# Four gate and value products of an attention chunk, from one float32 matmul each to three passes over split operands

## The chip, the cores and the metric

The kernel runs on one core of a Trainium2 chip. TensorE (PE) multiplies, VectorE (DVE), ScalarE (ACT) and GpSimd (POOL) do elementwise work, and SyncE (SP) issues transfers. The metric is the device time of one execution in microseconds, lower is better. Three runs of the kernel before gave 1155.25 us as the median (1154.32 to 1161.18).

## What is computed

Eight chunks of 512 tokens by 128 features pass through two model layers. Layer 0 is a feed-forward part with LoRA experts, a gated attention, and the same feed-forward part again; layer 1 is a mixture of experts, a softmax attention, and the mixture again. The change is in layer 0's attention, whose core is:

```python
h = _layernorm(x, ln1_g, ln1_b)
v = h @ Wv + bv
log_f = log_sigmoid(h @ Wf + bf);  log_i = log_sigmoid(h @ Wi + bi)
o = sigmoid(h @ Wo + bo)
scores = exp(log_i^T + cumsum(log_f) - cumsum(log_f)^T + causal)
attn = (scores / (sum(scores) + 1e-6)) @ v
x = x + o * attn;  x = x + mlp(layernorm(x))
```

The kernel computes the scores' two sums as scans along the tokens: `den` from the two gates, `num` from the gates and the values.

## The kernel before, in words

**Slots.** Layer 0 is written out by hand in slots. Slot `m` does the main feed-forward work of one chunk in one of the two feed-forward parts (m = 0 to 15), and beside it one step each of other chunks: chunk `m - 3` is at its gates (`a_gate`), chunk `m - 4` at its normalisation (`a_norm`), chunk `m - 5` at the first half of its small MLP (`a_up`), chunk `m - 6` at the second (`a_down`), and from m = 9 on chunks are sorted for the experts of layer 1 (`r_...`). So the gates run in slots 3 to 10. Every engine has its own list of steps per slot; the order within an engine is fixed by that list, and semaphores tie the engines together. A slot of the middle takes some 45 us. After the slots, from about 680 us on, come the experts and the softmax attention of layer 1, which the change does not touch.

**The passes.** `mm3` already does the feed-forward products in three matmuls of the type float32r (a shorter float that is kept in four bytes): the high part of the weights by the high and by the low part of the moving operand, then the low part of the weights by the high part. All other products are plain float32 matmuls, which the trace shows as two records each.

**The gates.** In slot `m`, PE transposes the normalised chunk into the shared bank `BSIDE` early in the slot (`a_T`), ACT evicts it with scale and bias to `hT`, and PE reads `hT` near the end of the slot, in four products into the same bank (`a_gate(0)` to `a_gate(3)`: input gate, forget gate, output gate, values). ACT evicts three of them with a sigmoid (`a_gates`); DVE reads the fourth in `a_scans`, which runs the `den` scan, the product `iv` and the `num` scan. Other PE steps stand between the gates: `up(1)` and half of `value(0)`, then `down(2)` and `down(3)`.

**The shared bank.** In the next slot PE's `a_den`, eight tiny matmuls (1x1), turns the row `den` into columns in that bank. It waits for the `num` scan and for the `hT` eviction of the following chunk, since that empties the bank. Behind it on PE stand `h(3, 2)`, `pre_T` and `a_back`. ACT evicts what `pre_T` writes (`tT` and its rounded copy), then normalises into `h2` (`a_mid_norm`), and DVE's `a_mix` waits for that; so DVE's work of the slot starts from there.

**DVE and POOL.** DVE's `act(k)` are two operations, bank by `sil` and then `act` by the mask `wT`. POOL adds (`total`), takes differences and raises the variances to the power -1/2 (`a_mid_scale` and others). DVE's `a_leaky(0)` late in the slot is followed on ACT by `a_square(0)`, `a_mid(2)`, `mask(2)`, `mask(3)`; PE's `up(0)` waits for `mask(3)`, DVE's `masked(0)` for `up(0)` and for POOL's `mask_diff`. 

Of the kernel before, what the change touches and what calls it, by code (L numbers as in the profile page):

```python
# [69 lines left out]
def build(nc, d, out):  # L70
    with ExitStack() as ctx:
        def sb(name, shape, dt=F32):
            return ctx.enter_context(nc.sbuf_tensor(name, shape, dt))

        def sem(name, per_item=1):
            return Sem(ctx.enter_context(nc.semaphore(name)), per_item)
# [10 lines left out]
        bank = [ctx.enter_context(nc.psum_tensor(f"bank{i}", [P, S], F32)) for i in range(8)]  # L87
# [9 lines left out]
        vecs = sb("vecs", [P, 8]); bif = sb("bif", [P, 2]); wif = sb("wif", [P, 2])  # L97
        wi_b = sb("wi_b", [P, P]); wf_b = sb("wf_b", [P, P])
        wv = sb("wv", [P, P]); wo = sb("wo", [P, P])
# [20 lines left out]
        gsum = [sb(f"gsum{i}", [P, S]) for i in range(2)]  # L120
        r1 = sb("r1", [P, S]); r2 = sb("r2", [P, S]); oT = sb("oT", [P, S])
        w1, w3, b1, b3 = act_[0]
# [6 lines left out]
        hT = sb("hT", [P, S])  # L129
        gi = sb("gi", [P, S]); gf = sb("gf", [P, S]); go = sb("go", [P, S])  # L130
        iv = sb("iv", [P, S]); num = sb("num", [P, S]); den = sb("den", [P, S]); oaT = sb("oaT", [P, S])
        denc = sb("denc", [P, 2, T])
# [4 lines left out]

        lower = sb("lower", [P, P]); lower_bf = sb("lower_bf", [P, P], BF16); ones_bf = sb("ones_bf", [P, P], BF16); ones = sb("ones", [P, 1])
        token_i = sb("token_i", [P, NCH * T], I32); token = sb("token", [P, NCH * T])
# [33 lines left out]
        mxr = sb("mxr", [P, 2]); nmx = sb("nmx", [P, 2]); rs = sb("rs", [P, 2]); rsi = sb("rsi", [P, T])  # L173

        with nc.sbuf_tensor("split", [P, 29 * S], F32R) as split:
            def parts(n, width=S):
                return tuple(split[:, (n + k) * S:(n + k) * S + width] for k in range(2))
            w1s, w3s, b1s, b3s = parts(0), parts(2), parts(4), parts(6)
            a1s, a3s = (tuple(split[:, 8 * S + (k + i) * P:8 * S + (k + i + 1) * P] for k in range(2)) for i in (0, 2))
            ts = [parts(9), parts(11)]  # L180
            uas = [[parts(13 + 8 * p + 2 * i) for i in range(2)] for p in range(2)]
            uds = [[parts(17 + 8 * p + 2 * i) for i in range(2)] for p in range(2)]
# [21 lines left out]
        routing_constants, ranked, zrow_ready, rows_zeroed = sem("routing_constants", 8 + E), sem("ranked"), sem("zrow_ready"), sem("rows_zeroed")  # L204
        prod_ready, prod_saved, scaled, spread, weight_high, weight_low = (
            sem("prod_ready"), sem("prod_saved"), sem("scaled"), sem("spread"), sem("weight_high"), sem("weight_low"))

# [9 lines left out]

        bn_a, stat_a, rstd_a, normed_a, ynT_a, hT_saved = (
            sem("bn_a", 4), sem("stat_a"), sem("rstd_a", 2), sem("normed_a", 2), sem("ynT_a"), sem("hT_saved"))
        gates_ready, gates_saved, scan_steps, oa_ready = sem("gates_ready", 4), sem("gates_saved", 3), sem("scan_steps", 3), sem("oa_ready")  # L220
# [39 lines left out]

        SPLITS = [(a1s, a1, 1.0), (a3s, a3, 1.0), (w1s, w1[:, :], 1.0), (b1s, b1[:, :], LORA), (w3s, w3[:, :], 1.0), (b3s, b3[:, :], LORA)]

        def window(eng, row, first, n, most):
# [89 lines left out]
        def _(pe):  # L353
# [22 lines left out]
            def first_layer(s):  # L376
# [215 lines left out]
                def a_gate(i):  # L592
                    n = s.a_gate
                    if n is None:
                        return
                    pe.wait_ge(*hT_saved(n))
                    if i == 0:
                        if n == 0:
                            pe.wait_ge(spread.sem, 2)
                        if s.a_norm is not None:  # L600
                            pe.wait_ge(*z_ready(s.a_norm))
                        if s.a_down is not None:
                            pe.wait_ge(*xa_done(s.a_down))
                        if s.a_up is not None:
                            pe.wait_ge(*m_saved(s.a_up))
                        if s.r_pre is not None:
                            pe.wait_ge(*xnT_saved(s.r_pre))
                    else:
                        pe.wait_ge(*gates_saved(n, i))
                    mm(bank[BSIDE][:, :], (wi_b, wf_b, wo, wv)[i][:, :], hT[:, :], start=True, stop=True).then_inc(gates_ready.sem, 1)  # L610

# [165 lines left out]
        def _(act):  # L777
# [12 lines left out]
            def first_layer(s):  # L790
# [128 lines left out]
                def a_T():  # L919
                    n = s.a_gate  # L920
                    if n is None:
                        return
                    if n == 0:
                        act.wait_ge(weights_loaded.sem, 16 * len(loads))
                        for k, w in enumerate((wi_b, wf_b)):
                            af(w[:, :], wif[:, k:k + 1].to_broadcast([P, P]), ACT.Copy).then_inc(spread.sem, 1)
                    act.wait_ge(*ynT_a(n))
                    act.wait_ge(*gates_ready(n - 1))
                    af(hT[:, :], bank[BSIDE][:, :], ACT.Identity, bias=vecs[:, 1:2], scale=vecs[:, 0:1]).then_inc(hT_saved.sem, 1)

# [133 lines left out]
        def _(dve):  # L1064
# [28 lines left out]
            def first_layer(s):  # L1093
# [163 lines left out]
                def a_scans():  # L1257
# [249 lines left out]
        def _(pool):  # L1507
# [13 lines left out]
            def first_layer(s):  # L1521
# [73 lines left out]
                def a_product():  # L1595
# [135 lines left out]
```

## Time and profile before

| | |
|---|---|
| median of three runs | 1155.25 us (1154.32 to 1161.18) |
| the profiled execution | 1153.79 us, of it span 1152.1 us |
| PE busy | 969.3 us (84%) |
| DVE, ACT, POOL busy | 721.7, 498.7, 494.9 us |
| mean granted TensorE clock | 0.928 of 2.4 GHz |

The page of the profile has one line of tenths for each engine, in 40 slices of 28.8 us. PE stands at nine tenths in slices 2 to 23, that is through the slots. A PE record is longer than the step to the next one, since matmuls overlap in the array; so distances between starts are read here, not lengths. A value in brackets behind a row is the idle time of that engine just before it, and who ended it.

### The profile page before, as it was taken

Reading aid. Unit: us, or ns where it says so; the run is one execution under the profiler, and the core shown is the slowest. Engines: PE = TensorE matmul, PEld = TensorE weight load, DVE = VectorE, ACT = ScalarE, POOL = GpSimd, SP = SyncE. Lnnn points to the kernel's source line nnn. Section 1 sums busy time; section 2 is a strip of 40 time slices with the busy share of each in tenths; the row PEclk is TensorE's granted clock in tenths of the full one; section 3 lists DMA queues with packets and bytes.
Section 4 is the critical chain, followed back from the end, with each engine's and each line's share of the span. In section 5 each row is a group of like instructions: output and inputs, shape, how many; then the busy total and the mean of one; then the engine's idle time right before and its main releaser. Section 6 shows DMA issues by size and latency. Waiting matters only on the chain. (4 is left out here: it accounts for less than half of the span.)

```text
span 1152.1 us, 15196 instructions
## 1 busy us (share of the span) xinstructions
PE 969.3 (84%) x4224; PEld 674.8 (59%) x4224; DVE 721.7 (63%) x2206; ACT 498.7 (43%) x1007; POOL 494.9 (43%) x475
## 2 busy tenths in 40 slices
PE   3999999999999999989999975888488884448884
PEld 2666655656656556556667644777255563337663
DVE  4878777868778777777878753444345546534332
ACT  3433454655565565634533322444144453323441
POOL 2445555455454453536545652444400005724434
PEclk9999999999999999999999976999789995569997
DMA  5087000000000000000000022555400000125441
GB/s 165 1 345 295 1 1 0 1 1 1 1 1 1 1 1 1 1 1 10 3 8 10 11 72 64 172 155 163 125 21 1 1 1 17 38 63 170 147 142 49
DMA packets 42901, 65.11 MB, mean 57 GB/s; under 512 B 7154, under 2 KB 25122, under 8 KB 40641
## 3 DMA queue, kind: packets, MB, share of 16 engines
q1 hardware_dynamic: 37824, 55.59, 14.7%
q0 software_dynamic: 4992, 8.54, 2.2%
q8 instruction: 35, 0.57, 0.2%
q14 instruction: 50, 0.40, 0.1%
HBM read 37.20 MB, written 28.74 MB: 57 GB/s over the span
## 5 line engine op out<-in xcount | busy, mean ns | idle before, releaser
L362 PE MATMUL bank<-split 128*128 128x512 f32 x416 | 207.4, 498 | 15.7 <-ACT wT L837 8.3
L364 PE MATMUL bank<-split 128*128 128x512 f32 x416 | 165.4, 398 | 0.0
L363 PE MATMUL bank<-split 128*128 128x512 f32 x416 | 165.1, 397 | 0.0
L798 ACT ACTIVATE sil<-bank 128x512 f32<-128x512 f32 x128 | 76.6, 599 | 114.5 <-PE bank L364 106.6
L1537 POOL TENSOR_TENSOR gsum<-act 128x512 f32<-128x512 f32 x64 | 84.9, 1327 | 89.5 <-DVE act L1109 89.5
L412 PE MATMUL bank<-act,a 128*128 128x512 f32 x256 | 117.9, 593 | 0.0
L362 PEld LDWEIGHTS bank<-split 128*128 128x128 f32 x416 | 79.5, 191 | 58.9 <-issue 20.4
L714 PE MATMUL bank<-hT_e,e 128*128 128x256 f32 x368 | 93.0, 397 | 20.0 <-ACT hT_e L1015 18.9
L1105 DVE TENSOR_TENSOR act<-bank,sil 128x512 f32<-128x512 f32 x128 | 87.8, 686 | 21.2 <-PE bank L364 19.3
L363 PEld LDWEIGHTS bank<-split 128*128 128x128 f32 x416 | 79.9, 192 | 29.0 <-issue 18.8
L698 PE MATMUL bank<-xlT,e 128*128 128x256 f32 x368 | 92.3, 396 | 3.3 <-ACT xlT L1002 2.7
L1109 DVE TENSOR_TENSOR act<-act,wT 128x512 f32<-128x512 f32 x128 | 90.0, 703 | 4.4
L364 PEld LDWEIGHTS bank<-split 128*128 128x128 f32 x416 | 79.4, 191 | 18.3
L714 PEld LDWEIGHTS bank<-hT_e,e 128*128 128x128 f32 x368 | 68.1, 195 | 33.9 <-ACT hT_e L1015 24.4
L1651 POOL DMA_INDIRECT out<-ob,ids x46 | 45.2, 983 | 80.0 <-DVE ob L1446 71.1
L1651 POOL DMA_INDIRECT rows_out<-ob,ids x46 | 45.2, 983 | 76.5 <-DVE ob L1446 68.7
L1007 ACT ACTIVATE ob<-xin 128x128 f32<-128x128 f32 x92 | 40.3, 485 | 86.8 <-DMA out<-ob,ids 44.2
L698 PEld LDWEIGHTS bank<-xlT,e 128*128 128x128 f32 x368 | 69.7, 199 | 13.5 <-ACT xlT L1002 3.9
L412 PEld LDWEIGHTS bank<-act,a 128*128 128x128 f32 x256 | 47.7, 191 | 42.3 <-issue 34.9
L1640 POOL DMA_INDIRECT rows_in<-yw,slot_i x64 | 63.0, 984 | 21.0 <-issue 15.5
L1438 DVE TENSOR_SCALAR oT_e<-bank,eb2T 128x256 f32<-128x256 f32 x46 | 22.3, 484 | 79.3 <-PE bank L714 79.3
L422 PE MATMUL bank<-gsum,w 128*128 128x512 f32 x128 | 65.2, 599 | 0.5 <-POOL gsum L1537 0.5
(280 smaller groups left out, 1926.2 us busy)
## 6 DMA issues: line engine op xcount, KB each, us to landing
e<-e_dram SPq DMA_DIRECT2D x92, 256.0 KB, 3.1
rows_in<-yw SPq DMA_DIRECT2D x17, 1056.0 KB, 17.9
xin<-rows_in SPq DMA_DIRECT2D x46, 132.0 KB, 3.1
x<-rows_out SPq DMA_DIRECT2D x8, 256.0 KB, 4.7
rows_in<-yw,slot_i POOLq DMA_INDIRECT x64, 2.3
rows_out<-ob,ids POOLq DMA_INDIRECT x46, 2.3
out<-ob,ids POOLq DMA_INDIRECT x46, 2.3
act<-b_dram SPq DMA_DIRECT2D x2, 256.0 KB, 3.2
```

What stands on the lines that cost most here:

```text
L362: mm(dst, w[0], m[0], start=start, stop=False, **more)
L363: mm(dst, w[0], m[1], start=False, stop=False, **more)
L364: return mm(dst, w[1], m[0], start=False, stop=stop, **more)
L412: last = mm(bank[BV][:, :], a2[:, j, :], act_[e][j][:, :], start=j == 0, stop=j == J - 1)
L422: mm(bank[BOUT][:, :], w2[:, j, :], gsum[j % 2][:, :], start=j == 0, stop=False).then_inc(w2_used.sem, 1)
L698: last = mm(bank[2 * p + j // 2][:, (j % 2) * Q:(j % 2 + 1) * Q], w[:, rows(j)], xlT[p][:, :], start=True, stop=True)
L714: last = mm(bank[4][:, 0:Q], w[:, j, :], hT_e[p][:, j, :], start=j == 0, stop=j == J - 1)
L798: af(sil[(k - 1) % 2][:, :], bank[BH1[STEPS[k - 1][0] % 2]][:, :], ACT.Silu).then_inc(silu_done.sem, 1)
L1105: v.tensor_tensor(a[:, :], bank[BH3[j % 2]][:, :], sil[(k - 1) % 2][:, :], ALU.mult).then_inc(act_done.sem, 1)
L1109: v.tensor_tensor(a[:, :], a[:, :], wT[g % 2][e][:, :], ALU.mult).then_inc(weighted.sem, 1)
L1537: pool.tensor_tensor(out=gsum[j % 2][:, :], in0=act_[0][j][:, :], in1=act_[1][j][:, :], op=ALU.add).then_inc(summed.sem, 1)
L1651: pool.indirect_dma_start((rows_out, o)[n3 // NT], bass.IndirectOffsetOnAxis(ids[n3 % 4][:, q:q + 1], 0), ob[n3 % 4][:, q, :], None, bound ...
```

## The change

Each of the four gate and value products becomes `mm3`. The four weights are split once, in slot 3, by four ACT copies (the high parts, where two copies stood that spread the gates' weight columns) and four DVE operations (`gates_low`). The moving operand is split for each chunk: ACT evicts the bank a second time, rounded, into the first half of `hT_split`, and signals `hT_saved` only after that; POOL subtracts in a new step `a_low`, between `a_mid_scale` and `total(1)`. `hT_split` lies on the memory of `iv` and `r2`, so ACT's eviction now waits for the `num` scan of the chunk before. The gates wait for `hT_low`.

```diff
-        wi_b = sb("wi_b", [P, P]); wf_b = sb("wf_b", [P, P])
+        gates_w = sb("gates_w", [P, 8 * P], F32R)
...
+        with nc.sbuf_tensor("hT_split", [P, 2 * S], F32R) as hT_split:
+            hTs = hT_split[:, 0:S], hT_split[:, S:2 * S]
+        iv, r2 = sb("iv", [P, S]), sb("r2", [P, S])
...
+        GATES = [wif[:, k:k + 1].to_broadcast([P, P]) for k in range(2)] + [wo[:, :], wv[:, :]]
...
-                    pe.wait_ge(*hT_saved(n))
+                    pe.wait_ge(*hT_low(n))
...
-                    mm(bank[BSIDE][:, :], (wi_b, wf_b, wo, wv)[i][:, :], hT[:, :], start=True, stop=True).then_inc(gates_ready.sem, 1)
+                    mm3(bank[BSIDE][:, :], gate_w[i], hTs, True, True).then_inc(gates_ready.sem, 1)
...
-                        for k, w in enumerate((wi_b, wf_b)):
-                            af(w[:, :], wif[:, k:k + 1].to_broadcast([P, P]), ACT.Copy).then_inc(spread.sem, 1)
+                        for dst, w in zip(gate_w, GATES):
+                            af(dst[0], w, ACT.Copy).then_inc(gate_high.sem, 1)
                     act.wait_ge(*ynT_a(n))
                     act.wait_ge(*gates_ready(n - 1))
-                    af(hT[:, :], bank[BSIDE][:, :], ACT.Identity, bias=vecs[:, 1:2], scale=vecs[:, 0:1]).then_inc(hT_saved.sem, 1)
+                    act.wait_ge(*scan_steps(n - 1))
+                    for dst in (hT[:, :], hTs[0]):
+                        last = af(dst, bank[BSIDE][:, :], ACT.Identity, bias=vecs[:, 1:2], scale=vecs[:, 0:1])
+                    last.then_inc(hT_saved.sem, 1)
...
+                def gates_low():
+                    if s.a_gate != 0:
+                        return
+                    dve.wait_ge(weights_loaded.sem, 16 * len(loads))
+                    for n, (dst, w) in enumerate(zip(gate_w, GATES)):
+                        dve.wait_ge(gate_high.sem, n + 1)
+                        v.scalar_tensor_tensor(dst[1], w, 1.0, dst[0].bitcast(F32), ALU.mult, ALU.subtract).then_inc(gate_low.sem, 1)
...
                 r_rows(s.r_sort, BSIDE)
+                gates_low()
                 masked(0)
...
+                def a_low():
+                    n = s.a_gate
+                    if n is None:
+                        return
+                    pool.wait_ge(*hT_saved(n))
+                    if l is not None:
+                        pool.wait_ge(*r_ready(l))
+                    pool.tensor_tensor(out=hTs[1], in0=hT[:, :], in1=hTs[0].bitcast(F32), op=ALU.subtract).then_inc(hT_low.sem, 1)
...
                 a_mid_scale()
+                a_low()
                 total(1)
```

How the order changes is seen best on three engines. On PE, before, from the second gate of slot 3 to the next slot's first product:

```order
L610 MATMUL bank<-hT,wf_b 128x512 [waits gates_saved,hT_saved]
L422 MATMUL bank<-gsum,w 128x512 [waits summed]
L610 MATMUL bank<-hT,wo 128x512 [waits gates_saved,hT_saved]
L422 MATMUL bank<-gsum,w 128x512 [waits summed]
L610 MATMUL bank<-hT,wv 128x512 [waits gates_saved,hT_saved]
L362 MATMUL bank<-split 128x512 [waits silu_done,t_low]
```

The same place now:

```order
L367 MATMUL bank<-hT_split,gates_w 128x512 [waits gates_saved,hT_low]
L368 MATMUL bank<-hT_split,gates_w 128x512
L369 MATMUL bank<-hT_split,gates_w 128x512
L427 MATMUL bank<-gsum,w 128x512 [waits summed]
L367 MATMUL bank<-hT_split,gates_w 128x512 [waits gates_saved,hT_low]
L368 MATMUL bank<-hT_split,gates_w 128x512
L369 MATMUL bank<-hT_split,gates_w 128x512
L427 MATMUL bank<-gsum,w 128x512 [waits summed]
L367 MATMUL bank<-hT_split,gates_w 128x512 [waits gates_saved,hT_low]
L368 MATMUL bank<-hT_split,gates_w 128x512
L369 MATMUL bank<-hT_split,gates_w 128x512
L367 MATMUL bank<-split 128x512 [waits silu_done,t_low]
```

Each gate is three instructions in the place of one, and nothing else moved. On ACT, at the start of a slot, before (`L798` is `silu`, `L929` the eviction, `L808` and `L809` are `pre_T`'s two evictions, `L862` is `a_mid_norm`):

```order
L798 ACTIVATE sil<-bank 128x512 [waits h1_ready]
L929 ACTIVATE hT<-bank,vecs 128x512 [waits gates_ready,ynT_a]
L798 ACTIVATE sil<-bank 128x512 [waits act_done,h1_ready]
L808 ACTIVATE tT<-bank,normw 128x512 [waits h3_ready,t_low,ynT_f]
L809 ACTIVATE split<-bank,normw 128x512
L862 ACTIVATE h<-z,nb_z,sc_z 128x128 [waits h2T_ready,rstd_z]
```

and now:

```order
L803 ACTIVATE sil<-bank 128x512 [waits h1_ready]
L936 ACTIVATE hT<-bank,vecs 128x512 [waits scan_steps,gates_ready,ynT_a]
L936 ACTIVATE hT_split<-bank,vecs 128x512
L803 ACTIVATE sil<-bank 128x512 [waits act_done,h1_ready]
L813 ACTIVATE tT<-bank,normw 128x512 [waits h3_ready,t_low,ynT_f]
L814 ACTIVATE split<-bank,normw 128x512
L867 ACTIVATE h<-z,nb_z,sc_z 128x128 [waits h2T_ready,rstd_z]
```

The eviction has a second instruction and a further wait. On POOL, before, in the first third of a slot (`L1537` is `total`, `L1591` and `L1593` are `a_mid_scale`):

```order
L1537 TENSOR_TENSOR gsum<-act 128x512 [waits w2_used,weighted]
L1591 TENSOR_TENSOR sc_z<-sc_z,neghalf 128x4 [waits stat_z]
L1593 TENSOR_TENSOR nb_z<-sc_z,mv_z 128x4 [waits rstd_z]
L1537 TENSOR_TENSOR gsum<-act 128x512 [waits w2_used,weighted]
L1550 TENSOR_TENSOR sc_f<-sc_f,neghalf 128x4 [waits stat_f]
```

and now:

```order
L1554 TENSOR_TENSOR gsum<-act 128x512 [waits w2_used,weighted]
L1608 TENSOR_TENSOR sc_z<-sc_z,neghalf 128x4 [waits stat_z]
L1610 TENSOR_TENSOR nb_z<-sc_z,mv_z 128x4 [waits rstd_z]
L1628 TENSOR_TENSOR hT_split<-hT,hT_split 128x512 [waits r_ready,hT_saved]
L1554 TENSOR_TENSOR gsum<-act 128x512 [waits w2_used,weighted]
L1567 TENSOR_TENSOR sc_f<-sc_f,neghalf 128x4 [waits stat_f]
```

The new subtraction stands between `nb_z` and the second `total`.

## Rows read from the trace of the kernel before

**Rows 1.** The page, busy time by engine (us, share of the span, instructions):

```profile
PE 969.3 (84%) x4224; PEld 674.8 (59%) x4224; DVE 721.7 (63%) x2206; ACT 498.7 (43%) x1007; POOL 494.9 (43%) x475
```

**Rows 2.** Who waited for whom, PE, 160 to 485 us (total, times, longest):

```profile
PE bank L362 <- ACT wT L837: 5.4, 7, 2.5
PE bank L610 <- ACT gi L903: 2.0, 5, 0.4
PE bank L362 <- DVE ud L1173: 1.5, 1, 1.5
```

**Rows 3.** Timeline of PE, end of slot 7 (start, length, engine, line, operation):

```profile
328.76 1.88 PE L412 MATMUL bank<-act,a 128*128 128x512 f32 x4
330.47 1.02 PE L610 MATMUL bank<-hT,wi_b 128*128 128x512 f32 x2
...
334.29 1.10 PE L610 MATMUL bank<-hT,wf_b 128*128 128x512 f32 x2 [0.39 <-ACT gi L903]
...
338.22 1.10 PE L610 MATMUL bank<-hT,wv 128*128 128x512 f32 x2
...
339.39 0.40 PE L363 MATMUL bank<-split 128*128 128x512 f32 x1
339.62 0.40 PE L364 MATMUL bank<-split 128*128 128x512 f32 x1
...
343.85 1.05 PE L492 MATMUL bank<-ones,den 1*128 1x1 f32 x8
```

**Rows 4.** Timeline of ACT, slot 7 and the start of slot 8:

```profile
324.70 0.63 ACT L894 ACTIVATE msq<-msq 128x512 f32<-128x512 f32 x1 [0.63 <-DVE msq L1247]
...
326.13 0.60 ACT L835 ACTIVATE wT<-bank 128x512 f32<-128x512 f32 x1 [0.22 <-PE bank L467]
...
332.16 1.28 ACT L903 ACT_TABLE_LOAD   x1
...
335.42 0.69 ACT L903 ACTIVATE gf<-bank,bif 128x512 f32<-128x512 f32 x1 [1.28 <-PE bank L610]
...
342.57 0.78 ACT L929 ACTIVATE hT<-bank,vecs 128x512 f32<-128x512 f32 x1
```

**Rows 5.** Timeline of DVE, the scans at the same place:

```profile
339.41 1.62 DVE L1265 TENSOR_TENSOR_SCAN den<-gf,gi 128x512 f32<-128x512 f32 x1 [4.78 <-PE bank L610]
...
341.71 1.49 DVE L1268 TENSOR_TENSOR_SCAN num<-gf,iv 128x512 f32<-128x512 f32 x1
```

**Rows 6.** Timeline of DVE and POOL, two overlaps, in slots 11 and 7:

```profile
488.20 1.27 POOL L1529 TENSOR_TENSOR split<-tT,split 128x512 fp32r<-128x512 f32 x1 [3.26 <-ACT split L809]
488.34 1.68 DVE L1109 TENSOR_TENSOR act<-act,wT 128x512 f32<-128x512 f32 x1
...
308.59 1.26 POOL L1584 TENSOR_TENSOR x<-x,z 128x512 f32<-128x512 f32 x1
308.75 1.12 DVE L1078 SCALAR_TENSOR_TENSOR part_z<-part_z 128x4 f32<-128x4 f32 x1
```

**Rows 7.** Timeline of POOL and DVE, where the subtraction is put, slots 7 and 4:

```profile
313.90 0.20 POOL L1593 TENSOR_TENSOR nb_z<-sc_z,mv_z 128x4 f32<-128x4 f32 x1
314.38 0.69 DVE L1109 TENSOR_TENSOR act<-act,wT 128x512 f32<-128x512 f32 x1
...
181.89 1.30 POOL L1537 TENSOR_TENSOR gsum<-act 128x512 f32<-128x512 f32 x1
183.50 0.15 DVE L1163 TENSOR_TENSOR dlt<-mx 128x4 f32<-128x4 f32 x1
```

**Rows 8.** Timeline of PE in slot 10, and a stretch (PEclk is the granted clock):

```profile
435.75 1.02 PE L492 MATMUL bank<-ones,den 1*128 1x1 f32 x8 [1.00 <-ACT hT L929]
...
437.14 0.63 PE L363 MATMUL bank<-split 128*128 128x512 f32 x1
437.57 0.63 PE L364 MATMUL bank<-split 128*128 128x512 f32 x1
...
437.00:443.00 6.00, 6.00 (x20) 4.12 (x20) 2.39 (x6) 2.63 (x6) 1.27 (x1) 0.72 0.00 0
```

More of the change, by code:

```diff
@@ L97, in build @@
         vecs = sb("vecs", [P, 8]); bif = sb("bif", [P, 2]); wif = sb("wif", [P, 2])
-        wi_b = sb("wi_b", [P, P]); wf_b = sb("wf_b", [P, P])
+        gates_w = sb("gates_w", [P, 8 * P], F32R)
+        gate_w = [tuple(gates_w[:, (2 * i + k) * P:(2 * i + k + 1) * P] for k in range(2)) for i in range(4)]
         wv = sb("wv", [P, P]); wo = sb("wo", [P, P])
@@ L120, in build @@
         gsum = [sb(f"gsum{i}", [P, S]) for i in range(2)]
-        r1 = sb("r1", [P, S]); r2 = sb("r2", [P, S]); oT = sb("oT", [P, S])
+        r1 = sb("r1", [P, S]); oT = sb("oT", [P, S])
         w1, w3, b1, b3 = act_[0]
@@ L130, in build @@
         gi = sb("gi", [P, S]); gf = sb("gf", [P, S]); go = sb("go", [P, S])
-        iv = sb("iv", [P, S]); num = sb("num", [P, S]); den = sb("den", [P, S]); oaT = sb("oaT", [P, S])
+        num = sb("num", [P, S]); den = sb("den", [P, S]); oaT = sb("oaT", [P, S])
         denc = sb("denc", [P, 2, T])
@@ L136, in build @@
         mv_z = sb("mv_z", [P, T]); sc_z = sb("sc_z", [P, 2, T]); nb_z = sb("nb_z", [P, T])
-        lower = sb("lower", [P, P]); lower_bf = sb("lower_bf", [P, P], BF16); ones_bf = sb("ones_bf", [P, P], BF16); ones = sb("ones", [P, 1])
+        lower = wak; lower_bf = sb("lower_bf", [P, P], BF16); ones_bf = sb("ones_bf", [P, P], BF16); ones = sb("ones", [P, 1])
         token_i = sb("token_i", [P, NCH * T], I32); token = sb("token", [P, NCH * T])
@@ L204, in build @@
         routing_constants, ranked, zrow_ready, rows_zeroed = sem("routing_constants", 8 + E), sem("ranked"), sem("zrow_ready"), sem("rows_zeroed")
-        prod_ready, prod_saved, scaled, spread, weight_high, weight_low = (
-            sem("prod_ready"), sem("prod_saved"), sem("scaled"), sem("spread"), sem("weight_high"), sem("weight_low"))
+        prod_ready, prod_saved, scaled, gate_high, gate_low, weight_high, weight_low = (
+            sem("prod_ready"), sem("prod_saved"), sem("scaled"), sem("gate_high"), sem("gate_low"), sem("weight_high"), sem("weight_low"))
         bn_f, stat_f, rstd_f, normed_f, ynT_f = sem("bn_f", 4), sem("stat_f"), sem("rstd_f"), sem("normed_f"), sem("ynT_f")
@@ L216, in build @@
         out_ready, outT_saved, back_ready, xf_done = sem("out_ready"), sem("outT_saved"), sem("back_ready"), sem("xf_done")
-        bn_a, stat_a, rstd_a, normed_a, ynT_a, hT_saved = (
-            sem("bn_a", 4), sem("stat_a"), sem("rstd_a", 2), sem("normed_a", 2), sem("ynT_a"), sem("hT_saved"))
+        bn_a, stat_a, rstd_a, normed_a, ynT_a, hT_saved, hT_low = (
+            sem("bn_a", 4), sem("stat_a"), sem("rstd_a", 2), sem("normed_a", 2), sem("ynT_a"), sem("hT_saved"), sem("hT_low"))
         gates_ready, gates_saved, scan_steps, oa_ready = sem("gates_ready", 4), sem("gates_saved", 3), sem("scan_steps", 3), sem("oa_ready")
@@ L595, in a_gate @@
                         return
-                    pe.wait_ge(*hT_saved(n))
+                    pe.wait_ge(*hT_low(n))
                     if i == 0:
                         if n == 0:
-                            pe.wait_ge(spread.sem, 2)
+                            pe.wait_ge(gate_low.sem, 4)
                         if s.a_norm is not None:
```

## The prediction

> **What bounds the kernel now.** I read the page first: PE is busy 84% of the span [rows 1], and the tenths show nine or more all through the slots, the only part that the change touches. A busy PE is not yet a bound, so the second view is PE's list of waits over slots 4 to 10 (160 to 485 us): some 10 us in 325 [rows 2, 8]. The reader should see that PE is the bound there, and that it still waits at four places: at `up(0)` for the masks on ACT (`L837`), at the second gate for the first sigmoid (`L903`), once for DVE's `ud`, once at `a_den` for `hT`. A delay is paid in full at each place where PE waits already, or where the slack is smaller than the delay. Third come the timelines around the gates and `a_den` [rows 3 to 5], fourth those around the place where POOL gets its new operation [rows 6, 7].
>
> **The gates.** A float32 product takes 0.855 us of PE (two of them from 328.76 to 330.47), a float32r pass 0.23 us (339.39 to 339.62) [rows 3], so three passes take 0.69 us and 32 products save at most 32 x 0.165 = 5.3 us. Not all of it counts:
> - The first gate's saving is lost. The second gate waits for the first sigmoid, that one for its table load at 332.16 [rows 4], which stands on ACT behind the last square or `up_high(0)`, and not behind the gate. Only in slot 5, by the same view, does the load start right after the gate: -0.14 us.
> - The second and third gate are each followed by their sigmoid, on which the next gate waits: 334.29 to 338.22 is two periods of 1.96 us [rows 3]. From the gate's start to its sigmoid it is 1.13 us now (335.42 [rows 4]). With three passes it is about 0.33 + 0.23 to the start of the last one, 0.40 for its record, 0.03 to ACT: 0.99. Saved 2 x 0.14 in 8 slots: -2.2 us.
> - The fourth gate belongs to the next term.
>
> Sum **-2.4 us**, with ends -5.3 and -1.
>
> The Trainium skill (FP8 and Floating Point Precision, TensorE Precision Notes) says that true float32 takes four passes through the array, so three would take three quarters. By that the product would fall to 0.64 us, an estimate from that page, and the gates would give about 0.8 us more. The trace's passes are 0.23 apart, for their weight loads are in the stream too, and the sum goes by the trace.
>
> **The wait at `a_den`.** Now `a_den` starts 5.63 us after the fourth gate of the slot before (338.22 to 343.85 [rows 3]); it is just about not waiting, since `hT` was done at 343.35 [rows 4]. In the new kernel: 0.99 us from the gate's start to the scans (1.19 now, 339.41), 3.79 to the end of the `num` scan (341.71 + 1.49 = 343.20) [rows 5], 0.05 to ACT, which waits for it now, 0.68 for `hT` (0.78 less a tenth of overlap between neighbours), 0.78 for the second eviction [rows 4], 0.13 back to PE. Sum 6.42 us, 0.79 more than now. Six slots (4 to 9): +4.7. In slot 10 ACT is late on its own account (PE waits 1.00 us there already [rows 8]), so the second eviction adds 0.68. In slot 11 there is no eviction, and the scans come 0.2 sooner. Sum **+5.2 us**. What is queued behind `a_den` on PE is `h(3, 2)`, `pre_T` and `a_back`, and `pre_T` feeds the chain over ACT to `a_mix`, from which DVE's slot starts; so nothing absorbs it: both the bound engine and its follower shift. Lower end: if the scan wait were free, `a_den` could start 0.68 after today's 343.48, at 344.16, 0.3 late, less the 0.2 of the gate: +1 us in all. Upper end: the full 1.0 us seven times, +7.
>
> **POOL's subtraction.** It takes 1.27 us like its neighbours, and POOL has room. But in this trace a DVE operation whose inputs both lie in SBUF stands still while a POOL operation on 512 columns runs: `L1109` took 1.68 instead of 0.69 us when POOL had started 0.14 earlier, and a tiny `L1078` 1.12 [rows 6], where `L1163`, as small, takes 0.15 [rows 7]. The subtraction starts at 314.12, behind `nb_z`; `L1109` follows at 314.38 [rows 7], would stand until 315.39 and end at 315.94 in place of 315.07: +0.87 us on DVE. In slots 4 and 5 the subtraction falls on DVE work that reads PSUM, but it pushes `total` from 181.89 to 183.19, over `L1163` at 183.50 [rows 7]: +0.95. In slot 3, where nothing stands between the first `total` and the subtraction, the same reading gives 0.45.
>
> What of it reaches PE: DVE's chain runs without a gap up to `a_leaky(0)`, and behind that ACT has `a_square(0)`, `a_mid(2)` and the masks on which `up(0)` waits. In slots 3, 4 and 5 PE or DVE waits on that chain already (the 1.5 us in slot 4, the longest, 2.5 us, in slot 5 [rows 2]): 0.45 + 0.95 + 0.95. In slot 7 the masks have 0.22 us of slack [rows 4], and the same reading of the others gives 0 in slot 6, 0.2 in 8 and 9, 0.57 in 10: 0.9 + 0.6 + 0.7 + 0.5 + 0.25. Together 5.3 us. `gates_low`, four small operations before `masked(0)` in slot 3, would be hidden by DVE's wait for `mask_diff`, but falls on that very POOL operation: +0.4 us. Sum **+5.7 us**. Lower end 0, if the starts fall apart by the 0.26 us that decide it, upper 8 times 1.0.
>
> The Trainium skill (SBUF — State Buffer, Who interferes with whom) has this as an exclusive lock: whichever starts first keeps it for the whole instruction. By that rule, were `L1109` to start first, DVE would lose nothing there, and POOL would end 0.7 us later; but then `total` comes over `L1163`, as in slot 4, and DVE pays its 0.95 after all. No row shows that order.
>
> **The clock.** In slot 10 PE stood still for 1.00 us, did 1.0 us of 1x1 matmuls, and its passes came 0.43 us apart behind that, at a granted clock of 1.2 GHz; the mean from 437 to 443 us is 0.72 [rows 8]. The new stall at `a_den` makes nearly the same picture in slots 4 to 9. A fall costs what that one did: seven passes or transposes at 0.43 instead of 0.23, about 1.5 us. Whether it falls depends on how stall and clock happen to lie; slot 5 shows one fall after 2.5 us, slot 4 none after 1.5. I take two of six: **+3.0 us**, ends 0 and 9.
>
> **Hidden.** Two more ACT copies and 0.2 us each in slot 3 lie in a gap of 1 us before `hT`. The second silu of a slot comes 0.7 us later, and what needs it waits for `h(3, 2)`, which comes 1 us later. Semaphore waits that are met already cost no gap in these rows. Nothing after 680 us changes.
>
> **Sum.** -2.4 + 5.2 + 5.7 + 3.0 = +11.5 us on the profiled execution's 1153.8: **1165 us**. That execution stands 1.5 us below the median of the three runs. A change of under 1% (11.6 us) can't be told from none in this kernel.
>
> **Rivals.**
> - *The collisions fall apart or are absorbed, and the clock holds.* Against the sum: the port's 0.26 us margin. For it: half the waits that POOL's operation brings would be shadowed by the stall at `a_den`, if PE's delay exceeds DVE's. -2.4 + 5.2 + 3 = +6, 1157 to 1162 us. Chance 0.27.
> - *Slower by more than 1%: the clock falls at most stalls.* Place: behind `a_den` in slots 4 to 10; price 1.5 us each, at six 9 us: 1171 us. It decides from four falls on. For it: slot 10 shows the same pattern with the fall. Against: the other long waits did not all bring one. Chance 0.16.
> - *The passes win.* Place: the gates. If ACT's second eviction and the wait for the scan hid behind `h(1, 2)`, and the port did not matter, the gates' -2.4 to -5.3 would stand alone: 1149 to 1152, up to 1156 with a little of the rest. Against it: `a_den` has no slack to hide 0.8 us in. Chance 0.12.
>
> The forecast has 0.45. Its own range is 1162 to 1168. Holding 8 in 10 takes the first rival's upper part and the second's lower: **1156 to 1172 us**. Faster by over 1% would need 11.5 us, twice what all gates can give: 0.02. Slower by over 1% (above 1166.8) takes the second rival and a third of the forecast: 0.31. Within 1%: 0.67.
>
> **What the profile afterwards would show.** PE's list of waits has `a_den` behind ACT's `L936` in slots 4 to 10 with 0.9 us each, 6 to 7 us in total. The distance from a gate's first pass to its sigmoid is near 1.0 us, and from sigmoid to sigmoid 1.82. `L1109`'s successor beside the subtraction takes about 1.5 us, and DVE's `dlt` 1.1 in slots 4 and 5. The wait of `up(0)` for the masks grows from 5.4 to 9 us or more. Clock: two falls more between 160 and 430 us. The prediction fails if the eviction starts before the `num` scan ends, if the DVE operations keep their 0.69 us, or if PE makes up for the stall later in the slot.

## The result, and the profile after

The changed kernel takes 1169.65 us (1165.53 to 1171.15, 4 runs) beside 1155.26 (1154.32 to 1161.18, 4 runs): ratio 1.0108, interval 1.0065 to 1.0151. The profiled execution took 1170.37 us, its span 1168.6. Ratios are to the kernel before on the same chip, with a 95% interval. In a row of a wait, the three numbers are the total in us, how often, and the longest.

PE's line of the page beside [rows 1]: the 32 further instructions are the three passes (a float32 matmul counted as two records).

```profile
PE 976.3 (84%) x4256; PEld 685.7 (59%) x4256; DVE 728.4 (62%) x2210; ACT 504.0 (43%) x1017; POOL 505.7 (43%) x483
```

Who waited for whom, PE, 160 to 485 us (beside [rows 2]):

```profile
PE bank L497 <- ACT hT_split L936: 8.1, 7, 1.7
PE bank L367 <- ACT wT L842: 6.0, 7, 2.1
PE bank L367 <- ACT gi L908: 2.3, 4, 0.6
PE bank L367 <- DVE ud L1181: 1.8, 1, 1.8
```

One line is new and large, `a_den` (`L497`) behind the second eviction, seven times. The masks' line hardly grew. The end of slot 7, timeline of all engines (beside [rows 3 to 5]):

```profile
342.34 0.47 PE L367 MATMUL bank<-hT_split,gates_w 128*128 128x512 f32 x1 [0.61 <-ACT gi L908]
...
343.31 0.69 ACT L908 ACTIVATE gf<-bank,bif 128x512 f32<-128x512 f32 x1 [1.12 <-PE bank L369]
...
344.14 0.47 PE L367 MATMUL bank<-hT_split,gates_w 128*128 128x512 f32 x1
...
345.95 0.47 PE L367 MATMUL bank<-hT_split,gates_w 128*128 128x512 f32 x1
...
346.40 1.30 POOL L1582 TENSOR_TENSOR split<-ua,split 128x512 fp32r<-128x512 f32 x1 [3.28 <-ACT split L851]
...
346.98 1.81 DVE L1273 TENSOR_TENSOR_SCAN den<-gf,gi 128x512 f32<-128x512 f32 x1 [4.52 <-PE bank L369]
...
349.47 1.49 DVE L1276 TENSOR_TENSOR_SCAN num<-gf,iv 128x512 f32<-128x512 f32 x1
...
351.07 0.78 ACT L936 ACTIVATE hT<-bank,vecs 128x512 f32<-128x512 f32 x1 [0.78 <-DVE num L1276]
...
351.75 0.77 ACT L936 ACTIVATE hT_split<-bank,vecs 128x512 fp32r<-128x512 f32 x1
...
352.66 1.02 PE L497 MATMUL bank<-ones,den 1*128 1x1 f32 x8 [1.06 <-ACT hT_split L936]
```

The gates come 1.80 us apart (1.96 before) and a gate reaches its sigmoid in 0.97 us (1.13). ACT now waits for the scan, evicts twice, and PE has stood still for 1.06 us. POOL and DVE in the same slot, and DVE in slot 4 (beside [rows 6, 7]):

```profile
186.41 0.89 DVE L1171 TENSOR_TENSOR dlt<-mx 128x4 f32<-128x4 f32 x1
...
321.54 1.30 POOL L1628 TENSOR_TENSOR hT_split<-hT,hT_split 128x512 fp32r<-128x512 f32 x1
321.86 1.53 DVE L1117 TENSOR_TENSOR act<-act,wT 128x512 f32<-128x512 f32 x1
```

`L1117`, the multiplication by the mask (`L1109` before), takes 0.84 us more than alone; about 1.5 us was foreseen, 1.53 came. `dlt` takes 0.74 us more, where 0.95 was foreseen. The 6 us behind each `a_den` of slots 4 to 10 (stretch, length, busy PE, PEld, DVE, ACT, POOL, then the granted clock):

```profile
168.00:174.00 6.00, 5.66 (x24) 4.68 (x25) 4.21 (x12) 1.95 (x4) 0.26 (x1) 0.72 0.01 3
212.00:218.00 6.00, 5.80 (x24) 4.52 (x25) 3.39 (x8) 2.71 (x7) 0.82 (x1) 0.72 0.00 0
259.00:265.00 6.00, 5.56 (x28) 4.07 (x29) 3.62 (x9) 3.26 (x8) 1.24 (x2) 1.00 0.01 3
306.00:312.00 6.00, 5.96 (x29) 4.23 (x30) 3.23 (x8) 3.18 (x7) 1.27 (x1) 1.00 0.01 3
352.00:358.00 6.00, 5.34 (x23) 4.53 (x24) 3.85 (x9) 2.25 (x5) 0.33 (x1) 0.72 0.01 3
400.00:406.00 6.00, 5.65 (x24) 4.61 (x25) 3.77 (x10) 2.35 (x6) 0.32 (x1) 0.72 0.01 3
448.00:454.00 6.00, 5.28 (x23) 4.50 (x24) 3.71 (x14) 1.88 (x4) 0.00 (x0) 0.72 0.01 3
```

A stretch of full speed has 1.00; 0.72 is the mean of a stretch that spends a part of its 6 us at 1.2 GHz. So the clock falls behind `a_den` in five of seven. In the trace of before only slot 10 shows it [rows 8]. Each of the two traces has one more fall in slot 5, late in the slot (at 236 and 242 us), which does not stand behind `a_den`.

**The measure for all runs.** `a_den` stands once in each slot on PE, so the distance between two of its starts is the price of a slot. I read it from each trace; the medians then say whether the sum holds. Slot 7 to 8 is the clean one: only the rows marked * have a fall of the clock in it. The column "slots 4 to 11" runs from `a_den` of slot 4 to that of slot 11.

| kernel | slot 7 to 8 | slots 4 to 11 | median us (runs) | ratio, interval |
|---|---|---|---|---|
| before | 45.32 | 316.76 | see text | 1 |
| changed | 46.62 | 328.02 | 1169.65 (4) | 1.0108, 1.0065 to 1.0151 |
| float32 gates, all costs | 46.90 | 329.62 | 1174.28 (4) | 1.0149, 1.0078 to 1.0220 |
| passes alone | 45.02 | 312.73 | 1152.76 (10) | 0.9962, 0.9927 to 0.9997 |
| subtraction on DVE | 47.86* | 326.70 | 1164.43 (10) | 1.0085, 1.0051 to 1.0118 |
| own memory | 45.78 | 317.09 | 1159.49 (10) | 1.0044, 1.0018 to 1.0071 |
| stall filled | 46.59 | 322.54 | 1163.33 (10) | 1.0039, 1.0012 to 1.0066 |
| before, POOL subtraction | 45.60 | 317.48 | 1159.78 (10) | 0.9999, 0.9963 to 1.0036 |
| copy made in SBUF | 45.49 | 316.61 | 1156.29 (10) | 0.9984, 0.9949 to 1.0019 |
| all mended | 45.02 | 312.87 | 1154.33 (12) | 0.9965, 0.9937 to 0.9992 |
| before, scan wait | 45.68 | 315.86 | 1156.04 (12) | 1.0010, 0.9980 to 1.0040 |
| changed, repeated | 47.91* | 328.92 | 1170.16 (6) | 1.0131, 1.0086 to 1.0175 |

The experiments ran on three chips. The kernel before took 1156.69 us beside the rows 3 to 6 of the table (25 runs), 1159.0 beside the next four (35), 1158.15 beside the last two (17). So a median is compared with another chip's only by way of the ratios. Medians are of all runs, while the ratios leave disturbed ones out (the largest is an execution of 2016.86 us of the kernel before with POOL's subtraction), so they are not always the quotient of the medians.

### The profile page after: what moved, and what is told of

The parts are those of the page before. It is cut to its first block and busy times, and to the rows that moved or that the text cites. A ratio compares the mean times of both kernels' runs of the same rounds, so it can differ in the third digit from the quotient of the medians.

```text
span 1168.6 us, 15291 instructions
## 1 busy us (share of the span) xinstructions
PE 976.3 (84%) x4256; PEld 685.7 (59%) x4256; DVE 728.4 (62%) x2210; ACT 504.0 (43%) x1017; POOL 505.7 (43%) x483
## 5 line engine op out<-in xcount | busy, mean ns | idle before, releaser
L367 PE MATMUL bank<-split 128*128 128x512 f32 x416 | 201.3, 484 | 17.5 <-ACT wT L842 8.9
L369 PE MATMUL bank<-split 128*128 128x512 f32 x416 | 165.8, 399 | 0.0
L368 PE MATMUL bank<-split 128*128 128x512 f32 x416 | 165.2, 397 | 0.0
L1117 DVE TENSOR_TENSOR act<-act,wT 128x512 f32<-128x512 f32 x128 | 92.8, 725 | 4.4
```

Source lines behind the costliest of these rows:

```text
L367: mm(dst, w[0], m[0], start=start, stop=False, **more)
L368: mm(dst, w[0], m[1], start=False, stop=False, **more)
L369: return mm(dst, w[1], m[0], start=False, stop=stop, **more)
L1117: v.tensor_tensor(a[:, :], a[:, :], wT[g % 2][e][:, :], ALU.mult).then_inc(weighted.sem, 1)
```

## The experiments

**Costs without the gain: float32 gates in the changed kernel.**

```diff
-                    mm3(bank[BSIDE][:, :], gate_w[i], hTs, True, True).then_inc(gates_ready.sem, 1)
+                    mm(bank[BSIDE][:, :], (wi_b, wf_b, wo, wv)[i][:, :], hT[:, :], start=True, stop=True).then_inc(gates_ready.sem, 1)
...
+                        for k, w in enumerate((wi_b, wf_b)):
+                            last = af(w[:, :], wif[:, k:k + 1].to_broadcast([P, P]), ACT.Copy)
```

> The changed kernel with its four products put back to one float32 matmul each on hT; the second eviction, its wait for the num scan, the subtraction on POOL and the weight splits all stay (their results are not read). So this has the costs without the gain. My theory, that the gates give back 2.4 us: 1171 to 1172 us if the changed kernel is at 1169 on this chip. Rival A, every one of the 32 products counts its 0.165 us: 1174 to 1175. Rival B, the shorter gates give nothing: 1169. The distance from the start of a gate to its sigmoid should be back at 1.13 us, and from sigmoid to sigmoid at 1.96.

1174.28 us. Timeline of PE:

```profile
307.07 1.02 PE L499 MATMUL bank<-ones,den 1*128 1x1 f32 x8 [1.03 <-ACT hT_split L942]
...
353.97 1.02 PE L499 MATMUL bank<-ones,den 1*128 1x1 f32 x8 [1.03 <-ACT hT_split L942]
```

46.90 us, 0.28 more than with the passes: in eight slots 2.2, the two gates of 0.14 us that the sum has. The median of 1174.28 us (1164.08 to 1180.32) is what rival A named, but four runs that spread over 16 us can't tell 2 us from 5. The slot can: all four gates would have made it 0.66 us longer. From a gate's start to its sigmoid it is 1.14 us again (343.34 to 344.48), and 1.97 from gate to gate.

**The gain without the costs.** No second eviction after the first chunk, no scan wait, no subtraction.

```diff
-                    act.wait_ge(*scan_steps(n - 1))
-                    for dst in (hT[:, :], hTs[0]):
+                    for dst in (hT[:, :], hTs[0])[:2 if n == 0 else 1]:
...
-                a_low()
```

> Three passes per gate, but the moving operand is never split: the passes of all chunks read the rounded copy of chunk 0, as high and as low part, so the products are not those of the reference. No second eviction after chunk 0, no wait for the scan, no subtraction on POOL. This has the gain without the costs. My theory: 2.4 us below the kernel before, about 1153 us. Rival A, all 32 products count: 1150. Rival B, a different way the slots fall together eats it: 1155.

1152.76 us. Timeline of PE:

```profile
297.30 1.05 PE L498 MATMUL bank<-ones,den 1*128 1x1 f32 x8
...
342.32 1.05 PE L498 MATMUL bank<-ones,den 1*128 1x1 f32 x8
```

45.02 against 45.32: -0.30 from the other side too. The passes do pay, about 2.4 us. (The sum over slots 4 to 11 is 4.0 less than before's; 2.0 of it is slot 10, where this trace has no fall. The interval of the ratio holds 0.3 to 8 us less.)

**The subtraction moved off POOL**, to DVE before `masked(0)`.

```diff
+                    v.tensor_tensor(hTs[1], hT[:, :], hTs[0].bitcast(F32), ALU.subtract).then_inc(hT_low.sem, 1)
...
-                    pool.tensor_tensor(out=hTs[1], in0=hT[:, :], in1=hTs[0].bitcast(F32), op=ALU.subtract).then_inc(hT_low.sem, 1)
```

> The changed kernel with the subtraction of the low part moved from POOL to DVE, right before masked(0), where DVE idles 1.4 to 2 us. My theory, that POOL's subtraction costs 0.25 to 0.95 us in each of eight slots by standing in the way of DVE: 5 to 6 us less than the changed kernel, about 1163 to 1164, and the multiplication by the mask beside a_mid_scale back at 0.69 us, dlt back at 0.15 us. Rival, that these delays are absorbed behind the stall at a_den: within 1 us of the changed kernel.

1164.43 us; by the ratios it is 0.2 to 0.5% (3 to 5 us) less than the two timings of the changed kernel, with intervals that overlap. The trace's slots 4 to 11 give 1.3 less only. The clock fell behind `a_den` in five of the seven, as it did there. What was expected of DVE came: the multiplications by the mask are back at 0.69 us and `dlt` at 0.15. But the place is not free either; timeline of POOL and DVE in slot 3, and a row of PE's waits, 160 to 485 us:

```profile
153.03 1.32 POOL L1584 TENSOR_TENSOR mdT<-mT 128x512 f32<-128x512 f32 x1
153.14 1.75 DVE L1285 TENSOR_TENSOR hT_split<-hT,hT_split 128x512 fp32r<-128x512 f32 x1
...
PE bank L367 <- ACT gi L908: 3.9, 5, 1.1
```

In slot 3 the subtraction collides with POOL itself (0.69 us in the other seven), and PE waits 3.9 us for the first sigmoid in place of 2.3. In slots 7 and 8, with a fall in each, this kernel takes 47.86 and 47.83 us and the changed kernel in its repeated run 47.91 and 48.01, with a fall in each too: next to the stall and the fall, moving the subtraction gained 0.05 to 0.18 us a slot. This run does not size the port; the pairs below do.

**The split operand in memory of its own**, so that ACT need not wait for the scan; the second eviction stays.

```diff
+        hT_high = sb("hT_high", [P, S], F32R)
...
-                    act.wait_ge(*scan_steps(n - 1))
```

> The changed kernel with the rounded high part in memory of its own, so that ACT's eviction does not wait for the num scan (three small tables are moved behind the split buffers to make room). The second eviction stays in front of a_den. My theory: a_den waits 0.3 to 0.4 us in place of 1.06, which is 0.65 us less in six slots, so 4 us, and with the shorter stall the four new stretches at 1.2 GHz go too, 1.5 us each, of which slack takes a part: 1160 to 1162. Rival, the clock does not follow the stall: 4 us less only, about 1165.

1159.49 us. Timeline of PE:

```profile
345.15 1.02 PE L499 MATMUL bank<-ones,den 1*128 1x1 f32 x8 [0.26 <-ACT hT_high L937]
```

The stall is 0.26 instead of 1.06 us, the slot 45.78 instead of 46.62, and no window behind `a_den` in slots 4 to 10 shows a fall, not even that of slot 10, where the stall is 1.74 us. The rival's 1165 is out.

**The rounded copy off the bank too**: ACT copies `hT` in SBUF after the second `silu`, so `a_den` waits for one eviction as before. Only the POOL subtraction is left of the costs.

```diff
-                    for dst in (hT[:, :], hTs[0]):
-                        last = af(dst, bank[BSIDE][:, :], ACT.Identity, bias=vecs[:, 1:2], scale=vecs[:, 0:1])
-                    last.then_inc(hT_saved.sem, 1)
+                    af(hT[:, :], bank[BSIDE][:, :], ACT.Identity, bias=vecs[:, 1:2], scale=vecs[:, 0:1]).then_inc(hT_saved.sem, 1)
...
+                    act.wait_ge(*hT_saved(n, 1))
+                    af(hTs[0], hT[:, :], ACT.Copy).then_inc(hT_saved.sem, 1)
```

> The kernel with the rounded part in its own memory, and beyond that the rounded part copied from hT on ACT after the second silu, so that a_den waits for one eviction only; the subtraction stays on POOL. My theory: no wait at a_den in slots 4 to 9, 1.0 us in slot 10 as in the kernel before, no stretch at 1.2 GHz there, and what is left is the port (+5) less the gates (-2.4 to -4): 1 to 3 us above the kernel before. Rival, the copy delays pre_T's evictions on ACT and thereby DVE's chain: 4 us or more above it.

1156.29 us. Timeline of PE and DVE:

```profile
298.35 1.05 PE L499 MATMUL bank<-ones,den 1*128 1x1 f32 x8
...
314.25 1.46 DVE L1124 TENSOR_TENSOR act<-act,wT 128x512 f32<-128x512 f32 x1
...
343.84 1.05 PE L499 MATMUL bank<-ones,den 1*128 1x1 f32 x8
```

45.49, so the second eviction alone costs 0.29 (45.78 - 45.49), and eviction and wait together 1.1 (46.59 - 45.49). The collision is all there, 1.46 us. Yet the 1 to 3 us above the kernel before did not come: the ratio is 0.9984 (0.9949 to 1.0019), and slots 4 to 9 take 0.3 us more than before's, or about 1.2 without a fall late in slot 5 that only the trace of before has (its price follows below). With six slots of gates at -0.30, that leaves 3 us for the port, not 5.

**And the subtraction off POOL**, to DVE between `act(2)` and `a_mix`, on the memory of `oaT`.

```diff
                 act(2)
+                a_low()
                 a_mix()
...
-                a_low()
```

> All three mended: own memory for the high part, the rounded copy from hT off the bank, and the subtraction on DVE in front of a_mix, where DVE idles 1.8 us; its result lies where oaT will be written later in the slot. My theory: the costs are gone and the gates' gain is left, 2.4 to 4 us below the kernel before, as the kernel with the passes alone. Rival, POOL's subtraction for pre_T (t_low) and DVE's now stand in each other's way, or DVE delays a_mix: no gain, within 1 us of the kernel before or above it.

1154.33 us, ratio 0.9965 (0.9937 to 0.9992): it beats both kernels, the one before by 1 to 7 us. The slots alone explain 2.4 us; of the 3.9 us in slots 4 to 11 the rest is mostly slot 10, where this trace too has no fall. Timeline of DVE and PE:

```profile
296.62 1.05 PE L500 MATMUL bank<-ones,den 1*128 1x1 f32 x8
...
300.97 0.69 DVE L1292 TENSOR_TENSOR hT_split<-hT,hT_high 128x512 fp32r<-128x512 f32 x1
...
341.64 1.05 PE L500 MATMUL bank<-ones,den 1*128 1x1 f32 x8
```

45.02, as with the passes alone, so the copy on ACT and the subtraction on DVE cost nothing there. (In slot 9 the subtraction collided with POOL, 1.76 us; the slot is no longer for it, 46.44 against 46.42 us with the passes alone.) Against the kernel above, POOL's subtraction costs 0.47 us in slot 7. Two waits tell where it gets through; first with it on POOL, then on DVE (PE, 160 to 485 us):

```profile
PE bank L369 <- ACT wT L844: 6.9, 7, 2.7
```

```profile
PE bank L370 <- ACT wT L845: 5.2, 7, 2.4
```

1.7 us for the masks in seven slots, of 0.77 lost on DVE in slot 7: some of it is absorbed on the way over ACT. Over slots 4 to 9 the two differ by 2.2 us. That is too little, since this trace has a fall late in slot 5 (235 us) and the one above has none. Such a fall is worth about 0.9 us, an estimate from the kernel before (45.34 us in slot 5, with one) and the one with the scan wait alone (44.79, without one, and 0.36 a slot dearer). With it, POOL's subtraction costs about 3.1 us.

**POOL's subtraction alone, in the kernel before.**

```diff
-                    pe.wait_ge(*hT_saved(n))
+                    pe.wait_ge(*hT_low(n))
...
+                    pool.tensor_tensor(out=hT_diff[:, :], in0=hT[:, :], in1=hT[:, :], op=ALU.subtract).then_inc(hT_low.sem, 1)
```

> The kernel before with one POOL subtraction of 128x512 added at the place of the change's, between a_mid_scale and total(1), on hT and into memory that nothing reads; the gates wait for it as they do in the changed kernel. The disputed port cost by itself. My theory: 4.5 to 5.5 us above the kernel before (0.9, 0.9, 0.9, 0.6, 0.7, 0.5 and 0.25 us in slots 4 to 10, 0.45 in slot 3), no new wait at a_den, and the multiplication by the mask beside it at 1.5 us in slots 6 to 10. Rival, absorbed on DVE: within 1.5 us of the kernel before.

1159.78 us, ratio 0.9999 with 0.4% to either side: the time alone can't see 3 us here. The trace does:

```profile
301.68 1.05 PE L493 MATMUL bank<-ones,den 1*128 1x1 f32 x8
...
317.19 1.04 POOL L1610 TENSOR_TENSOR hT_diff<-hT 128x512 fp32r<-128x512 f32 x1
317.52 1.26 DVE L1110 TENSOR_TENSOR act<-act,wT 128x512 f32<-128x512 f32 x1
...
347.28 1.05 PE L493 MATMUL bank<-ones,den 1*128 1x1 f32 x8
```

45.60 against 45.32; over slots 4 to 9 the distances sum to 2.3 us more, half of the 4.5 to 5.5 expected. This operation is not quite the change's: with `hT` as both inputs it takes 1.04 us and not 1.30, and DVE loses 0.57 us beside it and not 0.77. The two pairs then say the same: in slot 7, PE pays DVE's loss less 0.3 us (0.57 and 0.28 here, 0.77 and 0.47 above). In slot 3 the operation costs nothing in either pair. The kernels stand 1.58 us apart at DVE's `dlt` of slot 2, before any of it runs, and 1.60 at `a_den` of slot 4; the two above 0.58 and 0.64.

**The scan wait alone, in the kernel before.**

```diff
+                    act.wait_ge(*scan_steps(n - 1))
```

> The kernel before with one added line: ACT's hT eviction waits for the num scan of the chunk before, as in the change, and nothing else. My theory: hT starts 0.6 us later in slots 4 to 9, ends 0.8 us after the scan, and a_den waits about 0.25 us, so the distance between the a_den of two middle slots goes from 45.32 to about 45.6 us; no stall long enough for the clock; 1.5 to 2 us in all, less than the measurement can tell. Together with the second eviction alone (0.25 us of wait per slot in the kernel with own memory) this says that neither part costs much, and that the two in a row make the 1.06 us. Rival: the wait for the scan alone already brings the stall of about 1 us, and 8 us.

1156.04 us. Timeline of PE:

```profile
344.72 1.02 PE L492 MATMUL bank<-ones,den 1*128 1x1 f32 x8 [0.32 <-ACT hT L930]
```

A stall of 0.32 us, a slot of 45.68, 0.36 more: the wait and the eviction are small apart (0.36 and 0.29) and 1.1 together, for each uses up the same slack first. The slack would be the 0.37 us between `hT`'s end (343.35) and the last moment that would not delay `a_den` (343.85 less 0.13) in the trace of before [rows 3, 4]: 0.36 + 0.37 and 0.29 + 0.37, less one 0.37, make 1.02, near the 1.1 measured. The ratio, 1.0010 (0.9980 to 1.0040), can't tell so little.

**The stall filled.** The changed kernel with four further passes before `a_den` in slots 4 to 10, their result overwritten.

```diff
+                    if s.a_gate is not None and g is not None and q is not None:
+                        pe.wait_ge(*u_masked(q - 1))
+                        for k in range(4):
+                            mm(bank[BPRE][:, :], w1s[0][:, rows(k)], ts[g % 2][0], start=True, stop=True)
```

> The changed kernel with four extra float32r matmuls on PE in front of a_den in slots 4 to 10 (0.92 us, into the bank that pre_T empties next, their result is overwritten), so the stall of 1.06 us is filled with work and a_den starts when it did. My theory, that the stall followed by the 1x1 matmuls is what lets the clock fall: the stretches at 1.2 GHz behind a_den are gone in slots 4 to 9, and the time is 4 to 6 us below the changed kernel, though the kernel does more. Rival A, the clock stretches are there but hidden by other waits: the stretches go, the time stays within 1 us. Rival B, the stretches have another cause (the 1x1 matmuls alone): they stay, and the time too.

1163.33 us, ratio 1.0039 (1.0012 to 1.0066), against 1.0108 and 1.0131 of the changed kernel: PE does more, and the kernel is faster by 0.7 to 0.9%, 8 to 11 us. Timeline of PE, five of the seven stretches, and a row of PE's waits, 160 to 485 us:

```profile
349.60 1.09 PE L494 MATMUL bank<-split 128*128 128x512 f32 x4
350.84 1.02 PE L501 MATMUL bank<-ones,den 1*128 1x1 f32 x8
```

```profile
168.00:174.00 6.00, 5.86 (x29) 4.16 (x29) 5.07 (x16) 1.83 (x4) 1.27 (x1) 1.00 0.00 0
212.00:218.00 6.00, 6.00 (x29) 4.16 (x29) 3.11 (x8) 2.97 (x7) 1.27 (x1) 1.00 0.00 0
...
350.00:356.00 6.00, 5.86 (x31) 4.12 (x30) 4.04 (x9) 3.25 (x8) 1.25 (x2) 1.00 0.01 3
397.00:403.00 6.00, 5.86 (x30) 4.06 (x29) 3.90 (x10) 3.27 (x8) 1.25 (x2) 1.00 0.00 0
444.00:450.00 6.00, 5.26 (x27) 3.98 (x28) 3.73 (x14) 3.25 (x7) 0.83 (x1) 1.00 0.01 3
...
PE bank L367 <- ACT wT L846: 7.5, 7, 2.7
```

Where the changed kernel has 0.72, this one has 1.00, in all seven. Its slot 7 is as long (46.59), since `a_den` still starts when the eviction ends; only the clock differs. So the clock is worth 328.02 - 322.54 = 5.5 us in slots 4 to 11. That is six falls against one: the changed kernel has its sixth at 242 us, this one its only one at 198 us, late in slot 4, and neither stands behind `a_den`. No run has a stall that is not followed by the 1x1 matmuls, so what these add is not shown; without a stall they bring no fall.

**The changed kernel again**, for the number.

> The changed kernel itself, timed in five rounds beside the kernel before on this chip, to have its size against the experiments more exactly than four runs give it. My theory, from the sum as the traces now have it (gates -2.5, a_den +7, POOL's operation +4, clock +6): 1.011 to 1.013 of the kernel before, with three to six stretches at 1.2 GHz behind a_den, at other slots than in the first trace. Rival, the first four runs were high by chance: 1.006 or less.

1170.16 us (6 runs), ratio 1.0131. Its trace has the same stall of 1.07 us seven times, and falls behind three of them, in slots 7, 8 and 9, besides two elsewhere, at 198 us in slot 4 and 239 us in slot 5 (two of the stretches, granted clock third from the end):

```profile
306.00:312.00 6.00, 6.00 (x25) 4.73 (x26) 3.07 (x7) 1.96 (x5) 0.38 (x1) 0.72 0.00 0
...
450.00:456.00 6.00, 5.33 (x27) 3.98 (x28) 3.64 (x14) 3.27 (x7) 0.91 (x1) 1.00 0.01 3
```

Which stalls bring a fall changes from run to run; that they bring them does not. Four traces have the long stall at every `a_den` (the changed kernel twice, float32 gates, subtraction on DVE), with falls behind 5, 3, 4 and 5 of seven. In slots 4 to 9 of the eight other traces, where the stall is 0.34 us or less, none of 48 is followed by one.

## Why the prediction held, step by step

The range held: 1165 was forecast with 1156 to 1172 about it, and 1169.65 and 1170.16 were measured. The narrower range of 1162 to 1168 did not hold, and 1.0108 and 1.0131 lie above 1%, which had a chance of 0.31. Its sum is +11.5 us; from the pairs above it comes to about +12.3, and that the two are so near is luck in part:

| step | predicted | measured | from |
|---|---|---|---|
| gates | -2.4 | -2.4 | 8 x 0.30 |
| wait at `a_den` | +5.2 | +7.2 | 6 x 1.1, and 0.6 in slot 10 |
| POOL's subtraction | +5.7 | about +3.1 | 2.2 in slots 4 to 9, and 0.9 for the fall that hides it in slot 5 |
| clock | +3.0 | about +4.4 | 5.5 against the filled stall and 1.3 for that kernel's own fall, less 1.5 and 0.9 for the two of before |

The 1.3 us are slot 4 of the filled kernel, 43.61, less 41.19 + 1.1 (copy made in SBUF, and the stall); the 1.5 us are slot 10 of before, 48.00, beside 46.46 with POOL's subtraction and no fall. For the repeated run of the changed kernel the clock comes to about +5.3 in the same way. At `a_den` of slot 11 the two traces are 496.36 - 483.75 = 12.6 us apart, of which 0.4 was there before the gates ran (`dlt` of slot 2, 108.78 and 108.35): 12.2 against the sum's 12.3.

- **The gates: right.** The first one's gain is lost, two count. The trace decides against the estimate from the Trainium skill (FP8 and Floating Point Precision, TensorE Precision Notes): each of the two gave 0.14 to 0.16 us, near the forecast, and by that estimate it would have been 0.05 us more.
- **The wait: right in kind, too small.** From the fourth gate to `a_den` it is 352.66 - 345.95 = 6.71 us, forecast 6.42, before 5.63. PE's list of waits has 8.1 us there and not 6 to 7. Of the 0.29 missing, 0.19 is the `den` scan, 1.81 us long instead of 1.62. It is so in every kernel with the passes and in none with float32 gates. I had let it start 0.2 earlier and keep its length; its end came no sooner, so the fourth gate gave nothing. It starts 0.58 us into a POOL operation (346.40, 1.30 long), in the trace of before 0.74 into the same (338.67, 1.28 long). It ends 1.08 and 1.09 us after that operation does, so that DVE stands still until POOL is done fits both lengths; no run has the scan alone.
- **POOL's subtraction: this step failed, by nearly half.** The collision came, in slots 6 and 7 with the length foreseen (1.51 and 1.53 for 0.69). It was shorter for `dlt` (0.89 for 1.1) and in slots 8 and 9 beside falls of the clock (0.92 and 0.82). What failed is the way to PE. In slot 7 I charged 0.6; the pairs show DVE's loss less 0.3, so 0.47. (In slots 8 and 9 the sum has 0.7 and 0.5, though one slack of 0.2 makes both 0.67.) In slot 3 I charged 0.45 and, for `gates_low`, 0.4, and nothing came. The four operations of `gates_low` took 0.29 us each, and the last began at 152.41, before POOL's large one at 152.52.
- **The sign for the masks' wait was wrong.** I expected 9 us or more. It is 7.5 us with the stall filled and no fall behind `a_den`, and 6.0 in the changed kernel. There it is 0.96 and 0.98 us in slots 6 and 7, but 0.47, as before, in slots 8 and 9, where PE comes late from the slow stretch. In the repeated run the falls hide less: 7.1 us. So a part of POOL's cost is shadowed, as the first rival had it, but behind the falls and not behind the stall.
- **The lock.** The Trainium skill (SBUF — State Buffer, Who interferes with whom) calls the port an exclusive lock, and the lengths agree: the mask's multiplication ends 0.55 us after POOL's operation, whether that takes 1.30 us (323.39 and 322.84 in the changed kernel) or 1.04 (318.78 and 318.23 in the kernel before with POOL's subtraction). I wrote that no row shows the other order. One of the kernel before fits it: POOL's second operation starts as DVE's `den` scan of [rows 5] gets going, and takes 2.22 us where the first takes 1.28 (timeline of POOL):

```profile
338.67 1.28 POOL L1565 TENSOR_TENSOR split<-ua,split 128x512 fp32r<-128x512 f32 x1 [3.60 <-ACT split L846]
339.90 2.22 POOL L1565 TENSOR_TENSOR split<-ud,split 128x512 fp32r<-128x512 f32 x1
```

- **The clock: the size failed.** Two falls of six were forecast; the traces have four new ones (slots 4, 5, 8, 9) and three. "It decides from four falls on" was the second rival's condition, met in the first trace, with 9 us at six and 1171 us; the cost per fall, 1.5, was at the upper end of what came (1.1 to 1.6). The truth lies between forecast and rival. POOL's step was 2.6 us too dear, clock and `a_den` 1.4 and 2.0 too cheap, so three errors left 0.8.
- **The rivals.** That the passes win needed `a_den` to hide 0.8 us, and it can't. Yet freed of its costs, the idea is the version that wins: what costs is where and when their operand is made.

Open: why one stall of 1.06 us is followed by a fall and the next is not. Slot 10 has a stall of 1.0 us or more in seven of the other traces, and a fall behind two of them; the longest of these, 1.74 us, has none. Open too is what came behind slot 11: the two profiled executions are 16.6 us apart, 12.6 of it at slot 11, 1.4 more up to the last `down`, and 2.6 in layer 1, which the change does not touch. Both are within what the runs scatter, and no run here assigns them.

## What to carry to other kernels

Before adding a second reader of a shared bank, look who waits for the bank to empty: here the rounding cost 0.29 us a slot at `a_den`, and 1.1 together with the wait for the memory that it was laid on, where a copy out of SBUF, a few steps later, cost nothing. A memory overlay is a wait too, and two small delays that use the same slack have to be priced together. Where PE is the bound, price a new stall of 1 us with the half-speed stretch that may follow it; where the stall can't be removed, filling it may pay. And before a small cost is read from two traces, look whether they already stand apart before the change's first instruction, and whether one has a fall that the other lacks.

## What the hardware showed

- A stall of 1.06 us before eight 1x1 matmuls was followed by a stretch at 1.2 GHz in 5, 3, 4 and 5 of 7 slots in four traces; with four passes in the gap in 0 of 7, and with stalls of 0.34 us or less in none of 48 (slots 4 to 9 of eight traces). A fall cost 1.1 to 1.6 us in these slots.
- A DVE multiplication of two SBUF inputs, 128x512, took 0.69 us alone and 1.53 or 1.26 beside a POOL subtraction of 1.30 or 1.04 us; it ended 0.55 us after POOL in both. Of a loss of 0.77 us, 0.47 reached the slot's length.
- Slots of equal work repeat within 0.05 us in one trace (45.05, 45.02, 45.04 with the passes alone) and within 0.11 in another (45.41, 45.32, 45.30, before), while whole runs of one kernel on one chip scatter over 20 us. A cost of 0.3 us a slot was readable only in the distances, and ten runs were not enough to see 3 us.
